# A transformer block with routed experts: where the last unit chooses, and whether the experts have a block of their own

## What is computed

```python
mod = silu(c) @ wmod                      # six rows for each of the 8 batches: sa, ca, ga, sb, cb, gb
h = layernorm(x) * (1 + ca) + sa
x = x + ga * attention(h)                 # 16 heads, causal, softmax
h = layernorm(x) * (1 + cb) + sb
x = x + gb * ffn(h)

# ffn: 32 experts of hidden width 256, 4 of them for each of the 8192 tokens, and one shared path
scores = sigmoid(flat @ gate_w.T)
scores_c = scores + bias_corr             # used to choose alone
# 8 groups of 4 experts; a group counts the sum of its best two; the best 4 groups stay;
# of their experts the best 4 are chosen; their weights are the scores, normalised, times 2.5
pos = (place of the token among those of its expert, in the order of the tokens)
valid = pos < 256                         # an expert takes at most 256 tokens
xe[e, pos] = flat[token]
ye = relu2(xe @ up_w[e].T) @ down_w[e].T
routed = sum over the token's 4 experts of weight * ye[e, pos], where valid
shared = relu2(h @ shared_up_w.T) @ shared_down_w.T
return routed + shared
```

## Time and profile before

| | us |
|---|---|
| runs (3) | 3039.84, 3039.95, 3051.76 |
| median | 3039.95 |
| the profiled execution | 3048.27 |
| its span | 3046.6 |
| TensorE busy | 2924.1 (96%) |
| VectorE busy | 2123.5 (70%) |
| GpSimd busy | 1836.0 (60%) |
| ScalarE busy | 1343.7 (44%) |

### The profile page before, as it was taken

One profiled execution on the slowest core, in us unless ns is written; L12 is line 12 of the kernel. 1 busy time (PEld: TensorE's weight loads), 2 busy tenths in 40 slices (PEclk: granted clock), 3 DMA queues, 4 the chain that ended last, 5 costly groups with the idle time before them and its releaser, 6 DMA issues. The chain is left out here.

```text
span 3046.6 us, 49829 instructions
## 1 busy us (share of the span) xinstructions
PE 2924.1 (96%) x16480; PEld 2170.5 (71%) x16480; DVE 2123.5 (70%) x5344; ACT 1343.7 (44%) x2436; POOL 1836.0 (60%) x1077
## 2 busy tenths in 40 slices
PE   8999999999999999999999899999999999969997
PEld 5788888766666666666666578878877788758775
DVE  6555555677777777777777588878878888736664
ACT  2222222166666666566666533223322332226664
POOL 1332223278788888788888146666657666645664
PEclk9999999999999999999999899999999999989998
DMA  7555554845655565555664332333232323138996
GB/s 259 193 204 192 180 184 173 237 104 136 134 123 114 129 135 132 113 114 121 136 138 120 120 115 74 108 97 101 80 101 94 111 73 108 60 114 212 227 230 129
DMA packets 281949, 420.54 MB, mean 138 GB/s; under 512 B 48463, under 2 KB 132687, under 8 KB 281742
## 3 DMA queue, kind: packets, MB, share of 16 engines
q1 hardware_dynamic: 259214, 384.22, 44.5%
q0 software_dynamic: 22528, 33.72, 5.9%
HBM read 263.38 MB, written 153.01 MB: 137 GB/s over the span
## 5 line engine op out<-in xcount | busy, mean ns | idle before, releaser
L1143 ACT ACTIVATE att_pt<-att_ps_p 128x512 f32<-128x512 f32 (+1 forms) x1024 | 525.2, 586 | 133.3 <-PE att_ps_p L1368 104.4
L238 DVE CUSTOM_DVE_ANT_0 att_ps_s<-att_ps_s,att_causal 128x512 f32<-128x512 f32 (+1 forms) x992 | 470.2, 503 | 138.7 <-PE att_ps_s L1283 138.3
L1283 PE MATMUL att_ps_s<-att_ks,att_qs 96*128 96x512 f32 x1488 | 510.3, 372 | 5.1 <-PEq L395 3.7
L1365 PE MATMUL att_ps_p<-att_qs,att_ks 98*128 98x512 f32 (+3 forms) x1536 | 506.9, 370 | 8.1 <-ACT att_pt L1143 7.8
L244 DVE TENSOR_REDUCE att_lower<-att_ps_s 128x1 f32<-128x512 f32 x496 | 340.0, 685 | 121.4 <-PE att_ps_s L1283 121.4
L1084 POOL TENSOR_TENSOR att_gathered<-att_gathered,att_pt 128x2048 f32<-128x2048 f32 (+1 forms) x92 | 388.3, 4221 | 41.3 <-ACT att_pt L1143 36.5
L1365 PEld LDWEIGHTS att_ps_p<-att_qs,att_ks 98*128 98x128 f32 x1536 | 272.9, 191 | 153.2 <-issue 106.1
L1077 POOL TENSOR_TENSOR att_pt<-att_pt 128x1024 f32<-128x1024 f32 (+2 forms) x153 | 331.2, 2165 | 79.0 <-PE att_ps_o L1309 53.1
L1671 POOL DMA_INDIRECT slot_info<-ffn_info,ffn_slot x256 | 275.6, 1076 | 99.3 <-issue 75.9
L1283 PEld LDWEIGHTS att_ps_s<-att_ks,att_qs 96*128 96x128 f32 x1488 | 276.8, 192 | 72.5 <-DVE att_rowmax L238 22.1
L567 POOL TENSOR_TENSOR qkv_x<-qkv_x,qkv_mod 128x512 f32<-128x512 f32 x60 | 83.5, 1392 | 369.6 <-DVE qkv_x L657 369.6
(11 more groups left out here) (311 smaller groups left out, 6561.8 us busy)
## 6 DMA issues: line engine op xcount, KB each, us to landing
att_qs<-qk_parts SPq DMA_DIRECT2D x96, 512.0 KB, 6.8
att_ks<-qk_parts SPq DMA_DIRECT2D x96, 512.0 KB, 12.7
qk_parts<-qkv_out_hi SPq DMA_DIRECT2D x128, 256.0 KB, 2.2
qk_parts<-qkv_out_lo SPq DMA_DIRECT2D x128, 256.0 KB, 2.4
qkv_x<-x SPq DMA_DIRECT2D x16, 1024.0 KB, 5.6
v_rows<-qkv_out_v SPq DMA_DIRECT2D x64, 256.0 KB, 2.3
att_vs<-v_rows SPq DMA_DIRECT2D x32, 512.0 KB, 16.1
o_parts<-att_o SPq DMA_DIRECT2D x64, 256.0 KB, 7.2
```

The source lines that it names most:

```text
L238: dve.tensor_tensor_reduce(part, part, self.causal[:, UNIT - (c1 - c0):UNIT], scale=1.0, scalar=MASKED, op0=ALU.add, op1=ALU.max, accum_ou ...
L1143: act.activation(tile(c)[:, h, col:UNIT], ps_p[(NPROB * prev.g + n) % NP][:, col:UNIT], ACT.Exp, scale=float(HD) ** -0.5).then_inc(exp_don ...
L1283: pe.matmul(bank("s", cur.g, i)[:, 0:c1 - c0], qs[cur.slot][0:STACK, h, t * P:(t + 1) * P], ks[cur.slot][0:STACK, h, c0:c1], start=True, s ...
L1365: last = pe.matmul(part[:, i * (UNIT - col):(i + 1) * (UNIT - col)], ks[prev.slot][:, h + i, kt * P:(kt + 1) * P], qs[prev.slot][:, h + i, ...
```

## The change

The diff, cut to its core. `stage_experts` becomes `experts_programs`: the same five programs, returned as functions and called at the end of each engine's program in the third stage, so that there is one block in place of two and no meeting of all engines between. The lines of the five programs that aren't shown are the same as before.

```diff
-XG_PAD = 4352
+XG_PAD = 4136
...
+Experts = namedtuple("Experts", "sync gpsimd scalar vector tensor")
+def experts_programs(nc, e_upT, e_downT, h2_dram, out, relay, fin_done):
...
         def gpsimd(pool):
...
-            for n in ring[1:]:
-                relay.gather(pool, n, n, h2_dram)
             for out_stored in relay.x_out:
                 pool.wait_ge(out_stored, CREDIT + 16 * NB)
             body(0, 0)
...
         def tensor(pe):
...
+                if isinstance(e, int) and e == -1:
+                    pe.wait_ge(fin_done, CREDIT + UT * NB * HALVES)
                 if live(e + 1):
...
+        return Experts(sync, gpsimd, scalar, vector, tensor)
...
 def stage_project_route_shared(...):
+    relay.ident, relay.x_out = late.ident, late.x_out
+    experts = experts_programs(nc, e_upT, e_downT, h2_dram, out, relay, late.fin_done)
...
-        DOWN_AT = {0: 0, 1: 1, 4: 2, 5: 3}
+        SCATTERED_AHEAD = TOPK
+        CHOSEN_AHEAD, PLACED_AHEAD = {0: (0, 1), 1: (2,), 2: (3,), 3: (4, 5)}, 4
+        DOWN_AT = {0: 0, 1: 1, 3: 2, 4: 3}
+        FIRST_CHOICE = {1: (1,), 5: (2,), 7: (3, 4, 5)}
...
 # sync: bias and bo ahead of the loads of the attention output
             end = LastGroup(GROUPS - 1)
+            sp.dma_start(bias_sb[:, :], bias[:, :].broadcast_to([P, NE])).then_inc(consts, 16)
+            sp.dma_start(bo_sb[:, :], bo[:, :].broadcast_to([P, D])).then_inc(consts, 16)
             load_o(0, 1)
...
             load_mod(0)
-            sp.dma_start(bo_sb[:, :], bo[:, :].broadcast_to([P, D])).then_inc(consts, 16)
-            sp.dma_start(bias_sb[:, :], bias[:, :].broadcast_to([P, NE])).then_inc(consts, 16)
...
             steps(sp, body)
+            experts.sync(sp)
 # gpsimd
             def body(b, half, more):
                 u = b * HALVES + half
+                if u == UNITS - 2:
+                    scatter(u, half, 0, SCATTERED_AHEAD)
                 if more:
                     modulate(*((b, 1) if half == 0 else (b + 1, 0)))
                 if half == 0 and not (isinstance(b, int) and b == LAST) or half == 1 and more:
                     normalise(u + 2)
+                scatter(u, half, SCATTERED_AHEAD if u == UNITS - 2 else 0, UT * TOPK)
                 if not more:
                     pool.wait_ge(up_done, CREDIT + UP * UNITS)
                     pool.iota(...)
-                scatter(u, half)
...
             pool.wait_ge(h2_out, CREDIT + 16 * UNITS)
-            relay.gather(pool, 0, 0, h2_dram)
+            for e in range(RELAY_RING):
+                relay.gather(pool, e, e, h2_dram)
+            experts.gpsimd(pool)
 # scalar
+                def scores():
+                    act.wait_ge(logit_done, CREDIT + u + 1)
+                    act.wait_ge(chosen_done, CREDIT + u)
+                    act.activation(score[:, :, :], logits[:, :, :], ACT.Sigmoid).then_inc(score_done, 1)
+                if u == 0 or not more:
+                    scores()
                 for n in range(UP):
...
                     square(n)
-                    if n == 0:
-                        act.wait_ge(logit_done, CREDIT + u + 1)
-                        act.wait_ge(chosen_done, CREDIT + u)
-                        act.activation(score[:, :, :], logits[:, :, :], ACT.Sigmoid).then_inc(score_done, 1)
+                    if n == 0 and u and more:
+                        scores()
...
+            experts.scalar(act)
 # vector
-            late.last_invert(LastGroup(GROUPS - 1), 1)
-            dve.wait_ge(consts, CREDIT + 48)
...
+                if u == 0:
+                    dve.wait_ge(consts, CREDIT + 48)
+                    choose(u, 0)
                 for n in range(UP):
+                    if u == 0 and n == 2:
+                        late.last_invert(LastGroup(GROUPS - 1), 1)
+                    if not more:
+                        for step in CHOSEN_AHEAD.get(n, ()):
+                            choose(u, step)
+                        if n == PLACED_AHEAD:
+                            give_slots(u, half)
                     dve.wait_ge(ahi_done, CREDIT + UP * u + n + 1)
                     dve.tensor_tensor(a_lo[:, n, :], ...).then_inc(alo_done, 1)
...
-                    for step in (n,) if more else (2 * n, 2 * n + 1):
+                    for step in FIRST_CHOICE.get(n, ()) if u == 0 else (n,) if more else ():
                         choose(u, step)
-                if u >= UNITS - 2:
+                if u == UNITS - 2:
                     give_slots(u, half)
...
+            experts.vector(dve)
 # tensor
-            def exact(bank, pairs, halfway=lambda: None):
+            def exact(bank, pairs, before_pair=lambda n: None):
                 for i, (a, c) in enumerate(pairs):
-                    if 2 * i == len(pairs):
-                        halfway()
+                    before_pair(i)
...
+            def logits_back(u):
...
-                                                 for k in range(DK)]).then_inc(up_done, 1)
-                    if n == 0:
...
+                                                 for k in range(DK)],
+                          lambda k: logits_back(u) if not more and n == 0 and k == DK // 2 else None).then_inc(up_done, 1)
+                    if n == 0 and more:
+                        logits_back(u)
...
-                pe.wait_ge(alo_done, CREDIT + UP * (u + 1))
+                if more:
+                    pe.wait_ge(alo_done, CREDIT + UP * (u + 1))
...
+                    def before_pair(n):
+                        if more and t == PT and 2 * n == UP:
+                            turn(u + 1, PT)
+                        if not more and t == 0:
+                            pe.wait_ge(alo_done, CREDIT + UP * u + n + 1)
...
             steps(pe, body)
+            experts.tensor(pe)
```

More of the change, by code:

```diff
@@ L1482, in stage_project_route_shared @@
         h2_out, x_out, scattered = late.h2_out, late.x_out, late.scattered
-        relay.ident, relay.x_out = ident, x_out
         UNITS = NB * HALVES
@@ L1663, in body, with scatter @@
                     pool.iota(relay.iota_i[:, :], pattern=[[1, NK]], base=0, channel_multiplier=0).then_inc(relay.iota_done, 1)
-                scatter(u, half)
-            def scatter(u, half):
+            def scatter(u, half, first, end):
                 pool.wait_ge(slot_done, CREDIT + u + 1)
                 pool.sem_inc(mark, 1)
-                for j in range(UT * TOPK):
+                for j in range(first, end):
                     pool.indirect_dma_start(
@@ L2025, in body @@
                     cols = slice(t * P, (t + 1) * P)
+                    def before_pair(n):
[3 more added lines that the diff above has]
+                            pe.wait_ge(alo_done, CREDIT + UP * u + n + 1)
                     exact(ps_m[t % RING][:, :], [((a_hi[:, n, cols], a_lo[:, n, cols]), (dn_hi[:, n, :], dn_lo[:, n, :]))
-                                                 for n in range(UP)],
-                          lambda: turn(u + 1, PT) if more and t == PT else None).then_inc(down_done, 1)
+                                                 for n in range(UP)], before_pair).then_inc(down_done, 1)
                     if more:
```

376 lines of the change are left out of this document (184 added, 192 removed).

## The result

| us | before | changed |
|---|---|---|
| median of the runs | 3039.89 (6) | 3021.74 (6) |
| lowest, highest | 3035.57, 3051.76 | 3017.71, 3032.24 |
| span of the profiled execution | 3046.6 | 3023.3 |

The ratio is 0.9943, 95% interval 0.9923 to 0.9963: a gain of 18.2 us, by the interval 11 to 23 us. The forecast was 24.3 less, 3015.7. The direction is right and 3021.74 lies within the range, but the forecast gain lies just outside the measured interval.

A forecast was written before the change was run, and what follows sets the result against it. TensorE was taken to bound units 1 to 14, and scatter-adds at 8.9 us an expert the experts; only their starts could move. 20.1 + 4.2 = 24.3 us below 3039.95 gave 3015.7, range 3008 to 3029.

The forecast's parts named there:

- Part 1: Last unit: choosing and placing ahead, among the activation tiles, makes VectorE's slots end 13.35 us sooner.
- Part 2: Last unit's 16 scatters stay in a row; 4 of unit 14's go into GpSimd's idle 15.41 us; no gain counted.
- Part 3: Into the experts: one block and gathers 1.3 us apart bring expert 1's turn 6.8 us sooner, beyond the slots' 13.35.
- lands 4.92 us later: Step for gather 1: its second DMA, started at 2717.2, keeps its earlier flight time and lands at 2722.1.
- the lower bound: Gain at expert 1's turn only 16 us, if the crowd of transfers flies 7.46 us and expert 2's turn is late.
- The first rival: Boundary's cost stays as code, or crowded transfers delay gathers 1 and 2; the 6.8 us don't come: 3022.5, chance 0.15.
- part 4: First unit: reordered loads, splits and choice start attend sooner, gaining 4.2 us.
- I walk the ring to attend at 1777.0: First unit: following VectorE's work through the activation tiles puts attend at 1777.0 against 1781.22, a 4.2 us gain.
- Slots not early: Rival, last unit: `sel` or the Relus hold the up products and slots keep their old pace: 3029, chance 0.08.
- Given back in the experts: Rival, expert stretch: DMA bytes set its end, so only some 5 us are left: 3035, chance 0.07.
- Slower by the loop's fetches: Rival, expert loop: code fetched at each back edge, 3.5 us or more in each of 7 passes: 3066, chance 0.04.

The follow-up runs named there:

- e8: Changed kernel with the first-unit order of e7 and the three edits against the crowd of e9: 3058.74 us on chip C, ratio 0.9931.
- e9: Changed kernel, first unit as before, expert 4's weights and gathers 2 and 3 held, two `out` tiles stored early: 3059.05 us on chip C, ratio 0.9931.
- e2: Changed kernel with the experts in a block of their own again and gathers 1 to 3 behind its start: 3007.81 us on chip A, ratio 0.9967.
- e7: Changed kernel with unit 0's choice behind later `a_lo`, nearly clear of GpSimd, last two steps at unit's end: 3062.09 us on chip B, ratio 0.9941.
- e1: Changed kernel with the first unit as before, last unit and one block kept: 3008.71 us on chip A, ratio interval 0.9946 to 0.9975.
- after_third: The changed kernel unaltered, run again as a control on chip C: 3065.01 us, ratio 0.9946 to the kernel before.
- after_again: The changed kernel unaltered, run again as a control on chip B: 3055.56 us, ratio 0.9919 to the kernel before.

## Why the prediction was right or wrong

**Part 1, 13.35 us: 12.0 in the profile, 9.9 from the order alone.** `slot` was forecast 20.3 us behind gateT (2685.7 - 2665.36); it came 21.5, and 19.9 on chip A. That walk was right within its rows. What was off is the row that it was taken from: the 3.02 us for which VectorE waits in the earlier trace rows aren't part of the order. There TensorE's count of product 2 rose 5.1 us behind its last matmul, and on chip A, where no count is late, early slots gain 9.9. No wait stood ahead of `places`, as forecast; 2.08 us stood ahead of the down product, where I said under 1.5, at no cost.

**Part 2, no term.** Right: the four scatters went into the idle time (15.41 us became 6.18), and the last unit's scatters ran at once.

**Part 3, 6.8 us: 2.5.** The gathers were 1.25 to 1.30 us apart, as said, and went out 6.3 us sooner behind `slot`. The step that failed is "lands 4.92 us later": the last row landed 8.8 us after the DMA went out, more than the 7.46 that I had named as the lower bound, since I took for the price of the crowd the worst flight of a row in which there was less of a crowd. The forecast said expert 1's turn 36 us behind `slot`; it was 41, and 36.8 to 37.2 with the weights and gathers 2 and 3 held and half of the store (e8, e9), which is 6.3 to 6.6 us sooner than in the kernel before. The sum also left out expert 0's turn, behind which expert 1's stands by at least 2.66 us. In the crowd gather 0 took 8.0 us to land, its turn came at 37.64, and 40.3 of the 40.96 us follow from that; gather 1's own landing made the last 0.7. So the mechanism was right, and what was mis-sized is the flight of the first gathers. The first rival had named this cause among two, "or the crowd of transfers delays gathers 1 and 2 by as much", and its time, 3022.5, is 0.8 us from the measured one. That is partly luck: it priced part 4 at 4.2. Its other cause, code fetched at a jump, has no support: without the boundary GpSimd idles only 0.30 us ahead of gather 1, and with it, in e2, 6.96 us; but e2 can't divide that time into meeting and code.

**Part 4, 4.2 us: none.** "I walk the ring to attend at 1777.0" is the step that failed. From the stage's first turn, the last `a_lo` ended at 43.4 us before (1778.0) and at 41.6 after (1771.86 + 1.39), 1.8 sooner, and behind it now stand 5.1 us of steps 3 to 5, as forecast, where there was a wait of 3.20 for `x`. The walk needed the last `a_lo` 6.1 us sooner. It had priced step 0 at 3.9 us; it took 4.95 (1747.06 to 1752.0), and the halves and splits right behind it, 1.6 to 2.3 us each where 0.69 and 1.22 are usual, took what was left. GpSimd was held as well: its sums, 1.29 us alone, took up to 2.15 there (one took 2.27 in the kernel before). The rule of the Trainium skill that I set beside the row (SBUF — State Buffer, on the engines' doors) said just this, that a VectorE op with two SBUF inputs and a GpSimd op hold each other up; it spoke against this part and I gave it 1 us. The trace agrees with its direction, and the price was larger: beside GpSimd the new order gains nothing, nearly clear of it 2.0 us (e7) and 2.5 us (e8) at the next gate.

**The rivals.** Slots not early: no, `slot` moved. Given back in the experts: no, 278.2 us before and 273.9 after, within the scatter. Slower by the loop's fetches: no, the adds run from 2740.19 to 3014.1, 8.8 us an expert. What the Trainium skill says of stalls at a branch (Runtime: NRT & Kernel Launch, Instruction fetch mechanics) can't be seen at work here in either direction.

**The sum.** 12.0 + 2.5 + 0.7 = 15.2 us in the profile where 24.3 were forecast, and 18.2 in the medians, whose interval holds it. The rest of the span's 23.3 is the start of the stage, units 1 to 14 and the experts, which the change doesn't touch. On chip A the changed kernel itself did not run; e1, which differs from it by a first unit worth nothing, gained 12.3 us there, by its interval 8 to 16.

## What to carry to other kernels

Before a wait in the profile becomes a term, ask whether the order explains it: one behind an engine whose own rows run on at full pace (here "<-remote") can belong to the chip or the execution, and so can the gain that is priced from it. A transfer issued sooner meets other neighbours; price its flight by what will be in the air then, and where its reader is on the path, hold back what nobody needs yet. Work moved into an idle stretch of VectorE is only cheap if GpSimd is idle there too.

## What the runs showed of the hardware that was not expected

The chips differ in the stretch that is TensorE's. Fourteen units (gateT of 1 to 15) took 831.9 to 832.0 us on chip A, 849.7 and 850.8 on that of the result, 884.7 to 905.6 on B and 878.8 to 888.5 on C. (The 905.6 is e7's profile, of its slowest run.) On A, here in e1, TensorE has no pause at all in it:

```profile
1820.00:2630.00 810.00, 810.00 (x3856) 658.81 (x3855) 665.20 (x1416) 267.12 (x469) 550.35 (x464) 1.00 0.30 95
```

On C, in after_third, it waits 13 times for `h`, 22.8 us in all, 4.3 at most:

```profile
PE ffn_ps_t L2189 <- POOL ffn_h L1851: 22.8, 13, 4.3
```

The late counts go with this. On chip A no rise of `up_done` is over 0.02 us late in any unit. In the two profiles of the result's chip 28 and 29 rises are over 0.2 us late, in the eight of B and C 38 to 43, up to 8.8 us, in nearly every one of units 1 to 14. That they cause the longer units is likely, since ScalarE waits for this count and VectorE and GpSimd, which make `h`, follow, but no run shows it.

Behind such a wait the clock can fall too. In after_again, on B, TensorE waited 3.85 us for `h`, and the granted clock (third number from the right) was 0.50 in the window from 2300 to 2304 and 0.90 in the next:

```profile
2298.79 1.12 PE L2189 MATMUL ffn_ps_t<-all_ident,ffn_h 128*128 128x128 f32 x4 [3.85 <-POOL ffn_h L1851]
2300.00:2304.00 4.00, 4.00 (x11) 3.03 (x11) 3.93 (x4) 0.54 (x1) 3.84 (x4) 0.50 0.00 0
2304.00:2308.00 4.00, 4.00 (x19) 3.27 (x18) 2.44 (x5) 0.00 (x0) 3.75 (x4) 0.90 0.47 173
```

On the chip of the result units 8 and 14 took 67.0 and 63.0 us where most others took 59.9, and unit 4 took 62.6 before and 61.2 after. On chip A all took 59.2 to 59.4 but for unit 14, at 61.8, so only unit 14's is the kernel's own. Why the others are longer there was not tried.
